# Gating the stream on GpSimd in the first phase, and adding x on TensorE in the projection

## The chip, the core and the metric

The kernel runs on one core of one Trainium2 chip. The core has five engines that each work through a list of instructions of their own: TensorE (PE in the profile, its weight loads PEld), VectorE (DVE), ScalarE (ACT), GpSimd (POOL) and SyncE (SP), which here issues most of the DMAs. They meet at semaphores. The metric is the device time of the whole kernel in microseconds; lower is better.

## What is computed

A layer with adaptive layer norm around two blocks: a full attention block, and two layers of local attention with a feed-forward part. B = 2, T = 2048, C = 256, so 32 tiles of 128 rows. The change is in the attention block's surroundings. Cut to what matters:

```python
mod = (_silu(L0_c) @ L0_wmod).reshape(L0_c.shape[0], 6, 1, -1)
sa, ca, ga, sb, cb, gb = (mod[:, k] for k in range(6))
ga = (2 * (ga >= 0) - 1) * jnp.maximum(jnp.abs(ga), 0.25)
h = _layernorm(x, axis=-1) * (1 + ca) + sa
x = x + ga * _L0_attn_ref(h, ...)            # attn(h) = h + out @ Wo.T
h = _layernorm(x, axis=-1) * (1 + cb) + sb
x = x + gb * _L0_ffn_ref(h, ...)             # two layers of local attention + feed-forward
```

So the stream behind the attention is x1 = x + ga * h + ga * (out @ Wo.T), and the input of the two layers is x2 = layernorm(x1) * (1 + cb) + sb. The product with ga in the last term sits in the weights: w_gated = Wo.T * ga.

## The kernel before

The 32 tiles are worked in 8 groups of 4 tiles (512 rows; a tile of a group in SBUF is 128 partitions x 4 x 256 numbers, 128x1024 in the profile). All data are float32. A float32 product on TensorE shows as two records in the trace. The phases run one after another, with a barrier between them: a short setup, the first phase (`qkv_phase`), the attention (`attention_phase`), the projection (`projection_phase`), and then for each of two layers a local attention and a feed-forward phase. Order within a phase is what the code writes for each engine: loops over groups, software-pipelined by hand, with a wait on a semaphore ahead of each step.

**First phase.** GpSimd loads a group of x (L284), then raises two variances to the power -0.5 (L287, 128x4). VectorE makes the statistics (L224, L229, L386), normalises (L393), multiplies and adds the modulation (L396, L401) to give h in `h_now`, makes its statistics (L404), normalises again into `hn` (L410). TensorE transposes `hn` (L332); ScalarE brings it back as `xnt` (L296) and copies h into `S.h1` (L298), which signals `h_kept`; VectorE waits for `h_kept` before it writes the next `h_now` (L401). TensorE makes the products for q and k (L343), v (L353) and the dot products (L363), VectorE rotates q and k (L418, L419, L424) and makes their low parts (L428). VectorE's list of a group n interleaves these: statistics of n + 1, then four rotations, with the steps `modulated`, `shifted` and `normed` (L393 to L410) of group n + 1 between them.

**Projection.** `S.h1` holds h. For each group n with buffer p = n mod 2: VectorE multiplies h by ga in place (L1092, `gate_x`, two groups ahead), GpSimd adds x, which SyncE fetched again into `x_again` (L1050, `add_x`, two groups ahead), TensorE multiplies the attention's output `ot` by `w_gated` into `y_ps` (L1080, two buffers), VectorE adds it (L1100, `residual`) and makes the statistics (L224, L229, L1105). GpSimd makes the power (L1054), VectorE the offset -mean * rstd (L1110, `centre`), ScalarE normalises (L1034), VectorE multiplies by 1 + cb (L1114, `modulate`), GpSimd adds sb (L1058, `shift`) into `S.x2`. SyncE sends x1 to HBM (L1011) behind each group's loads. Its list for group n is: wait for `x_added` of n - 2, fetch x (L1003), wait for `mm_done` of n - 2, fetch ot (L1007, two DMAs), wait for `x1_ready` of n - 2, send. ScalarE's queue loads the weights and tables of the next phase behind its second normalisation (`W.load_local`, L957 to L961).

Of the kernel before, what the change touches and what calls it, by code (L numbers as in the profile page):

```python
# [11 lines left out]
ALU = mybir.AluOpType  # L12
# [3 lines left out]
P = 128  # L16
# [216 lines left out]
def qkv_phase(nc, S, E, io):  # L233


    with ExitStack() as ctx:
# [23 lines left out]
        prime(nc, q)  # L260
        with nc.Block() as block:
# [18 lines left out]
            @block.gpsimd  # L280
            def _(pool):
                with pool.Fori(0, GROUPS) as n:
                    pool.wait_ge(q["x_used"], n + START)
                    pool.dma_start(xin[:, :, :], row_tiles(io["x"])[:, ds(n * GT, GT), :]).then_inc(x_in, 16)  # L284
                    for k, (given, done) in enumerate((("var1", "rstd1"), ("var2", "rstd2"))):
                        pool.wait_ge(q[given], n + 1 + START)
                        pool.tensor_tensor(rstd[:, k, :], var[:, k, :], S.half[:, 0:GT], ALU.pow).then_inc(q[done], 1)  # L287

            @block.scalar
            def _(act):  # L290
                def inputs(n):
# [6 lines left out]
                    act.activation(S.h1[:, ds(n * GT, GT), :], h_now[:, :, :], ACT.Copy).then_inc(q["h_kept"], 1)  # L298
# [75 lines left out]
            def _(dve):  # L374
                LINKS = 5

                def mod(n, s):
                    return S.mod[:, ds(n // GPB, 1), s, :].to_broadcast([P, GT, C])


# [591 lines left out]
def projection_phase(nc, S, W, io):  # L972

    with ExitStack() as ctx:
# [6 lines left out]
        offset, carrier = sb("offset", [P, 2, GT]), sb("carrier2", [P, 1])  # L981
        y_ps = ps("y_ps", [P, 2, GT, C])
        o_in, x_in = ([sem(f"p_{n}_in{k}") for k in range(2)] for n in "ox")
        names = "w w_ready x1_out x_gated x_added x1_ready mm_done var rstd offset_ready normed scaled x2_done chain".split()
# [11 lines left out]
        with nc.Block() as block:  # L996

            @block.sync
            def _(sp):
# [16 lines left out]
                with sp.Fori(1, GROUPS // 2) as i:  # L1016
                    for p in range(2):
                        n = 2 * i + p
                        sp.wait_ge(q["x_added"], n - 1 + START)
                        fetch_x(n, p)  # L1020
                        sp.wait_ge(q["mm_done"], n - 1 + START)
# [24 lines left out]
            def _(pool):  # L1046
                def add_x(n, p):
                    pool.wait_ge(x_in[p], 16 * (n // 2 + 1) + START)
                    pool.wait_ge(q["x_gated"], n + 1 + START)
                    pool.tensor_tensor(x1(n), x1(n), xin[:, p, :, :], ALU.add).then_inc(q["x_added"], 1)  # L1050

                def scale(n, p):
                    pool.wait_ge(q["var"], n + 1 + START)
                    pool.tensor_tensor(rstd[:, p, :], rstd[:, p, :], S.half[:, 0:GT], ALU.pow).then_inc(q["rstd"], 1)  # L1054

# [4 lines left out]
                add_x(0, 0)  # L1060
                add_x(1, 1)
                scale(0, 0)
                with pool.Fori(0, GROUPS // 2 - 1) as i:
                    for p in range(2):
                        n = 2 * i + p
                        add_x(n + 2, p)
# [7 lines left out]
            def _(pe):  # L1074
                def project(n, p, b):
                    pe.wait_ge(o_in[p], 16 * CC * (n // 2 + 1) + START)
                    pe.wait_ge(q["x1_ready"], n - 1 + P0 + START)
                    for t in range(GT):
                        for k in range(CC):
                            last = pe.matmul(y_ps[:, p, t, :], ot[:, p, k, t * P:(t + 1) * P], w_gated[:, b, k, :], start=k == 0, stop=k == CC - 1)  # L1080
# [9 lines left out]
            def _(dve):  # L1090
                def gate_x(n):
                    dve.tensor_tensor(x1(n), x1(n), mod(n, 2), ALU.mult).then_inc(q["x_gated"], 1)  # L1092

                def residual(n, p):
# [3 lines left out]
                    dve.wait_ge(q["x_added"], n + 1 + START)  # L1098
# [5 lines left out]
                                    lambda t: [S.h1[:, ds(n * GT + t, 1), :].rearrange("p t c -> p (t c)")]))  # L1104
                    dve.tensor_scalar(rstd[:, p, :], mv[:, p, :, 1], EPS, None, ALU.add).then_inc(q["var"], 1)  # L1105
                    c.closed()

                def centre(n, p):
                    dve.wait_ge(q["rstd"], n + 1 + START)
                    dve.scalar_tensor_tensor(offset[:, p, :], mv[:, p, :, 0], -1.0, rstd[:, p, :], ALU.mult, ALU.mult).then_inc(q["offset_ready"], 1)  # L1110
# [7 lines left out]
                gate_x(0)  # L1118
                gate_x(1)
# [815 lines left out]
```

## Time and profile before

| | us |
|---|---|
| median of 3 runs | 2889.11 |
| the runs | 2885.9 to 2897.32 |
| the profiled execution | 2896.74 |
| its span | 2894.7 |

Over the span TensorE is busy 88%, VectorE 76%, ScalarE 54% and GpSimd 19%. One execution was profiled; durations are read from it. Times on the axis are microseconds from the start of its span. In a timeline row the first number is the start, the second the busy time of the instructions on the row (x4 means four, merged), and square brackets hold the engine's idle time before them and what ended it.

### The profile page before, as it was taken

What the parts mean: (1) busy time and instruction counts of PE and PEld (TensorE: products, weight loads), DVE (VectorE), ACT (ScalarE), POOL (GpSimd) and SP (SyncE); (2) the same over time, 40 slices, a digit from 0 to 9 for tenths busy, and PEclk for the clock granted to TensorE, in tenths of its full rate; (3) what the DMA queues carried; (4) which work ended last, traced back from release to release, by engine and by line L of the source; (5) the groups of instructions that cost most, each with busy time, mean ns of one, the idle gap of its engine ahead of it and who ended that gap; (6) DMA issues with size and microseconds to landing.
All of it is one profiled execution on the core that took longest, in us unless ns stands there. A gap on an engine that the chain in (4) does not pass through costs nothing. (4 is left out here: it accounts for less than half of the span.)

```text
span 2894.7 us, 45406 instructions
## 1 busy us (share of the span) xinstructions
PE 2549.8 (88%) x14072; PEld 1542.4 (53%) x14072; DVE 2194.7 (76%) x4596; ACT 1558.3 (54%) x3447; POOL 563.3 (19%) x388
## 2 busy tenths in 40 slices
PE   4995999999999999943999999669969999995998
PEld 2443333333333333322677777458847777773877
DVE  4776999999999999846788888435558888883565
ACT  0221666766667667711666666434426666663443
POOL 0110010101101110134333333100013333330000
PEclk7997999999999999976999999889989999998999
DMA  2335244445444554244100000020020000001121
GB/s 85 110 110 140 84 134 109 124 127 141 119 112 124 127 138 118 75 160 133 51 9 9 9 8 7 30 101 17 15 60 9 8 9 9 9 4 37 57 62 40
DMA packets 123905, 204.92 MB, mean 71 GB/s; under 512 B 22560, under 2 KB 71008, under 8 KB 120400
## 3 DMA queue, kind: packets, MB, share of 16 engines
q1 hardware_dynamic: 109040, 163.96, 20.3%
q0 software_dynamic: 8832, 21.80, 2.6%
q10 hardware_dynamic: 5920, 17.75, 1.6%
q8 instruction: 58, 0.95, 0.1%
q14 instruction: 55, 0.45, 0.1%
HBM read 125.30 MB, written 54.26 MB: 62 GB/s over the span
## 5 line engine op out<-in xcount | busy, mean ns | idle before, releaser
L751 PE MATMUL o_ps<-probs,vx 128*33 128x512 f32 (+3 forms) x2560 | 545.4, 548 | 0.0
L802 ACT ACTIVATE probs<-st_ps 128x512 f32<-128x512 f32 (+3 forms) x640 | 339.2, 530 | 314.3 <-PE st_ps L736 180.7
L853 DVE SCALAR_TENSOR_TENSOR geo_x<-geo_rows,kp_t 128x512 f32<-128x512 f32 (+3 forms) x640 | 437.7, 708 | 4.0 <-ACT probs L804 4.0
L832 DVE TENSOR_REDUCE chunk_max<-a_ps 128x1 f32<-128x512 f32 (+3 forms) x640 | 358.9, 602 | 41.9 <-PE a_ps L719 35.3
L804 ACT ACTIVATE probs<-geo_x 128x512 f32<-128x512 f32 (+3 forms) x640 | 360.9, 564 | 12.9 <-DVE geo_x L859 12.9
L1227 PE MATMUL local_in_ps<-w_local,local_ht 128*128 128x512 f32 x1152 | 322.5, 417 | 9.7 <-ACT local_sq L1369 5.3
L1388 ACT ACTIVATE local_probs<-local_s_ps,local_bias,local_inv 128x256 f32<-128x256 f32 x512 | 282.6, 563 | 13.9 <-DVE local_bias L1483 13.9
L1663 PE MATMUL ff_ag_ps<-ff_ht_parts,w 128*128 128x512 f32 (+1 forms) x1056 | 259.9, 405 | 33.6 <-DVE ff_gate L1772 25.4
L719 PE MATMUL a_ps<-k,q 96*128 96x512 f32 (+3 forms) x640 | 237.6, 445 | 43.3 <-DVE chunk_max L832 35.6
L1395 ACT ACTIVATE local_pt<-local_pt_ps 128x512 f32<-128x512 f32 x256 | 152.4, 596 | 208.9 <-PE local_pt_ps L1285 200.8
L751 PEld LDWEIGHTS o_ps<-probs,vx 128*33 128x33 f32 x2560 | 124.2, 112 | 260.4 <-issue 186.9
L719 PEld LDWEIGHTS a_ps<-k,q 96*128 96x128 f32 x640 | 108.9, 198 | 266.4 <-DVE chunk_max L832 135.7
L1479 DVE TENSOR_REDUCE local_top<-local_s_ps 128x4 f32<-128x1024 f32 x128 | 156.8, 1225 | 122.3 <-PE local_s_ps L1271 122.3
L1663 PEld LDWEIGHTS ff_ag_ps<-ff_ht_parts,w 128*128 128x128 f32 (+1 forms) x1056 | 200.0, 192 | 88.7 <-DVE ff_gate L1772 33.8
L1227 PEld LDWEIGHTS local_in_ps<-w_local,local_ht 128*128 128x128 f32 x1152 | 207.6, 193 | 58.2 <-issue 18.8
L1490 DVE TENSOR_SCALAR local_probs<-local_probs,local_rden 128x256 f32<-128x256 f32 x512 | 223.0, 477 | 9.0
L1556 POOL TENSOR_TENSOR local_inv<-local_norm,half 128x16 f32<-128x16 f32 x64 | 186.4, 2912 | 174.9 <-DVE local_norm L1468 107.6
L734 PE MATMUL st_ps<-q,k 98*128 98x512 f32 (+3 forms) x640 | 217.8, 412 | 2.0 <-DMA q<-maxima 2.0
L1676 PE MATMUL ff_y_ps<-ff_w,ff_act_t 128*128 128x256 f32 x1152 | 149.6, 285 | 14.5 <-DVE ff_act_t L1778 13.8
L1295 PE MATMUL local_o_ps<-local_pt,local_v_ring 128*64 128x128 f32 x2048 | 154.6, 282 | 3.3 <-ACT local_pt L1395 3.1
L1285 PE MATMUL local_pt_ps<-ident,local_probs 128*128 128x128 f32 x1024 | 150.7, 280 | 6.2 <-DVE local_probs L1490 1.4
L1676 PEld LDWEIGHTS ff_y_ps<-ff_w,ff_act_t 128*128 128x128 f32 x1152 | 140.5, 190 | 21.2 <-DVE ff_act_t L1778 21.0
(171 smaller groups left out, 3848.8 us busy)
## 6 DMA issues: line engine op xcount, KB each, us to landing
geo_rows<-geo SPq DMA_DIRECT2D x64, 512.0 KB, 7.5
q<-q_parts SPq DMA_DIRECT2D x48, 256.0 KB, 4.2
k<-k_parts SPq DMA_DIRECT2D x48, 256.0 KB, 6.3
piece_lo<-in_pieces POOLq DMA_DIRECT2D x15, 768.0 KB, 5.9
weight_parts<-piece_hi SPq DMA_DIRECT2D x15, 768.0 KB, 3.4
weight_parts<-piece_lo SPq DMA_DIRECT2D x15, 768.0 KB, 6.0
raw<-out_t SPq DMA_DIRECT2D x128, 64.0 KB
shares_in<-shares SPq DMA_DIRECT2D x64, 128.0 KB, 4.6
```

The source lines that it names most:

```text
L719: ins = pe.matmul(slot[:, 0:width], q3[s][0:ROWS, it * P:(it + 1) * P], k3[s][0:ROWS, c * GTOK:c * GTOK + width], start=True, stop=not diag)
L734: ins = pe.matmul(out[:, off:GTOK], k3[s][:, j * P:(j + 1) * P], q3[s][:, g * GTOK + off:(g + 1) * GTOK], start=True, stop=not diag)
L751: ins = pe.matmul(o_ps[kind * HALF:kind * HALF + VW, g % 2, off:GTOK], vx[s][:, j, :], probs[:, i % PSLOTS, kind, off:GTOK], start=j == 0, ...
L802: act.activation(probs[:, s % PSLOTS, 0, off:GTOK], st_ps[:, (b * NB + s) % STBANKS, off:GTOK], ACT.Exp).then_inc(q["st_used"], 1)
L804: act.activation(probs[:, s % PSLOTS, 1, off:GTOK], geo_x[:, s % GSLOTS, off:GTOK], ACT.Exp).then_inc(q["probs_ready"], 1)
L832: dve.reduce_max(chunk_max[:, it, c:c + 1], a_ps[:, n % ABANKS, 0:width], AX.X).then_inc(q["a_used"], 1)
L853: ins = dve.scalar_tensor_tensor(out[:, off:GTOK], geo[:, 1, at], kp_t[:, j, ds(b, 1)].rearrange("p o -> p o"), geo[:, 0, at], ALU.add, AL ...
L1227: last = pe.matmul(in_ps[:, j, :], ht[:, p, a, k, :], w[:, b, k, j * INNER:(j + 1) * INNER], start=i == 0, stop=i == len(steps) - 1)
L1388: last = act.activation(probs[:, hd, :], s_ps[:, a, x % 2 * 2 * P:(x % 2 + 1) * 2 * P], ACT.Exp, bias=bias[:, hd:hd + 1], scale=inv[:, p, ...
L1490: last = dve.tensor_scalar(probs[:, hd, :], probs[:, hd, :], rden[:, hd:hd + 1], None, ALU.mult)
L1663: last = pe.matmul(ag_ps[0:rows, x % 2, half, :], w1[:, a, k, c0:c0 + rows], ht_parts[:, b, k, :], start=i == 0, stop=i == len(steps) - 1)
L1676: last = pe.matmul(y_ps[:, t, :], act_t[:, a, x, t * P:(t + 1) * P], w2[:, b, x, :], start=(x, i) == (0, 0), stop=x == HC - 1 and i == len ...
```

## The change

In the first phase ScalarE's copy of h into `S.h1` goes. In its place GpSimd multiplies `h_now` by ga into `S.h1` (`keep_gated`), in its list behind the load of the next group's x; the last group's stands behind the loop. `h_kept` is now signalled by it.

In the projection VectorE's `gate_x` and GpSimd's `add_x` go, with their semaphores. TensorE adds x: two products of the identity with `x_again` (128x512 each) open the accumulation in `y_ps`, and the products with `ot` go on in it. SyncE fetches x for group n behind `mm_done` of n - 2, with ot. The offset is made in two steps: VectorE writes -mean to `centre` (128x4), GpSimd multiplies it by rstd right behind the power.

```diff
             @block.gpsimd
             def _(pool):
-                with pool.Fori(0, GROUPS) as n:
+                def fetch(n):
                     pool.wait_ge(q["x_used"], n + START)
                     pool.dma_start(xin[:, :, :], row_tiles(io["x"])[:, ds(n * GT, GT), :]).then_inc(x_in, 16)
+
+                def scales(n):
                     for k, (given, done) in enumerate((("var1", "rstd1"), ("var2", "rstd2"))):
                         pool.wait_ge(q[given], n + 1 + START)
                         pool.tensor_tensor(rstd[:, k, :], var[:, k, :], S.half[:, 0:GT], ALU.pow).then_inc(q[done], 1)
+
+                def keep_gated(n):
+                    pool.wait_ge(q["h_ready"], n + 1 + START)
+                    pool.tensor_tensor(S.h1[:, ds(n * GT, GT), :], h_now[:, :, :], mod(n, 2), ALU.mult).then_inc(q["h_kept"], 1)
+
+                fetch(0)
+                scales(0)
+                with pool.Fori(1, GROUPS) as n:
+                    fetch(n)
+                    keep_gated(n - 1)
+                    scales(n)
+                keep_gated(GROUPS - 1)
...
-                    act.activation(S.h1[:, ds(n * GT, GT), :], h_now[:, :, :], ACT.Copy).then_inc(q["h_kept"], 1)
...
-                        sp.wait_ge(q["x_added"], n - 1 + START)
+                        sp.wait_ge(q["mm_done"], n - 1 + START)
                         fetch_x(n, p)
-                        sp.wait_ge(q["mm_done"], n - 1 + START)
                         fetch_o(n, p)
                         send(n - 2)
...
                 def scale(n, p):
                     pool.wait_ge(q["var"], n + 1 + START)
                     pool.tensor_tensor(rstd[:, p, :], rstd[:, p, :], S.half[:, 0:GT], ALU.pow).then_inc(q["rstd"], 1)
+                    pool.wait_ge(q["rstd"], n + 1 + START)
+                    pool.tensor_tensor(offset[:, p, :], centre[:, p, :], rstd[:, p, :], ALU.mult).then_inc(q["offset_ready"], 1)
...
-                        add_x(n + 2, p)
                         scale(n + 1, 1 - p)
                         shift(n, p)
...
                 def project(n, p, b):
+                    pe.wait_ge(x_in[p], 16 * (n // 2 + 1) + START)
+                    pe.wait_ge(q["x1_ready"], n - 1 + P0 + START)
+                    for t in range(0, GT, 2):
+                        pe.matmul(y_ps[:, p, t:t + 2, :], S.ident[:, :], xin[:, p, t:t + 2, :], start=True, stop=False)
                     pe.wait_ge(o_in[p], 16 * CC * (n // 2 + 1) + START)
-                    pe.wait_ge(q["x1_ready"], n - 1 + P0 + START)
...
-                            last = pe.matmul(y_ps[:, p, t, :], ot[:, p, k, t * P:(t + 1) * P], w_gated[:, b, k, :], start=k == 0, stop=k == CC - 1)
+                            last = pe.matmul(y_ps[:, p, t, :], ot[:, p, k, t * P:(t + 1) * P], w_gated[:, b, k, :], start=False, stop=k == CC - 1 and t % 2 == 1)
...
                     dve.wait_ge(q["normed"], n - 1 + P0 + START)
-                    dve.wait_ge(q["x_added"], n + 1 + START)
                     dve.wait_ge(q["mm_done"], n + 1 + START)
...
+                    dve.tensor_scalar(centre[:, p, :], mv[:, p, :, 0], -1.0, None, ALU.mult)
                     dve.tensor_scalar(rstd[:, p, :], mv[:, p, :, 1], EPS, None, ALU.add).then_inc(q["var"], 1)
...
-                        gate_x(n + 2)
-                        centre(n, p)
                         residual(n + 1, 1 - p)
                         modulate(n, p)
```

GpSimd in the first phase, before: the loop over groups is a load of x and two powers (an ISA row sets a register or a configuration).

```order
L282 ISA
L284 ISA
L284 DMA xin<-in_x 128x4x256
L286 REGISTER_ALU
L287 ISA
L287 TENSOR_TENSOR rstd<-var,half 128x4 x2
L282 REGISTER_ALU
L282 COMPARE_AND_BRANCH
```

The same loop after, with the instruction that follows it (line numbers are those of the changed file; x is S.h1).

```order
L300 ISA
L287 ISA
L287 DMA xin<-in_x 128x4x256
L296 ISA x2
L296 TENSOR_TENSOR x<-h_now,mod 128x1024
L291 REGISTER_ALU
L292 TENSOR_TENSOR rstd<-var,half 128x4 x2
L300 REGISTER_ALU
L300 COMPARE_AND_BRANCH
L296 TENSOR_TENSOR x<-h_now,mod 128x1024
```

A 128x1024 multiply now stands between the load and the two powers, and one more behind the loop.

GpSimd in the projection, before: the first half of the loop's body (x on L1050 is S.h1, on L1058 S.x2).

```order
L1050 ISA
L1050 TENSOR_TENSOR x<-x,x_again 128x1024
L1053 REGISTER_ALU
L1054 TENSOR_TENSOR rstd<-rstd,half 128x4
L1058 ISA x2
L1058 TENSOR_TENSOR x<-normed,mod 128x1024
```

And after:

```order
L1059 TENSOR_TENSOR rstd<-rstd,half 128x4
L1061 TENSOR_TENSOR offset<-centre,rstd 128x4
L1064 REGISTER_ALU
L1065 ISA x2
L1065 TENSOR_TENSOR x<-normed,mod 128x1024
```

The addition of x is gone and a 128x4 multiply stands behind the power.

TensorE in the projection after, the two halves of the loop's body; before there were only the groups of eight.

```order
L1083 MATMUL y_ps<-x_again,ident 128x512 x2
L1084 ISA
L1087 MATMUL y_ps<-w_gated,ot 128x256 x8
L1080 ISA
L1081 REGISTER_ALU
L1083 MATMUL y_ps<-x_again,ident 128x512 x2
L1084 ISA
L1087 MATMUL y_ps<-w_gated,ot 128x256 x8
```

Each group of eight products with `ot` now has two 128x512 products ahead of it.

## Rows read from the trace of the kernel before

**Rows 1.** Projection: busy us of PE, PEld, DVE, ACT, POOL; clock, DMA share, GB/s:

```profile
1265.00:1349.00 84.00, 34.15 (x128) 27.36 (x128) 62.97 (x124) 16.61 (x32) 52.40 (x24) 0.72 0.64 224
```

**Rows 2.** Timeline, one group of the first phase: start, us, instructions:

```profile
80.65 14.00 PE L343 MATMUL qk_ps<-xnt,w_qkv 128*128 128x512 f32 x32
...
84.57 0.69 DVE L418 SCALAR_TENSOR_TENSOR rot_c<-qk_ps,cos_t 128x512 f32<-128x512 f32 x1 [4.11 <-PE qk_ps L343]
...
95.43 1.01 POOL L287 TENSOR_TENSOR rstd<-var,half 128x4 f32<-128x4 f32 x1 [13.86 <-DVE var L404]
...
96.41 0.80 POOL L284 DMA_DIRECT2D xin<-in_x  x1
...
97.18 0.68 DVE L428 TENSOR_TENSOR lo<-qk,hi 128x512 fp32r<-128x512 f32 x1
...
97.78 1.38 DVE L410 TENSOR_SCALAR hn<-h_now,mv,rstd 128x256 f32<-128x256 f32 x4
...
102.80 1.88 PE L363 MATMUL v_ps<-qk,dirs 128*8 128x512 f32 x4 [1.42 <-ACT dots_sb L316]
...
104.61 1.98 PE L343 MATMUL qk_ps<-xnt,w_qkv 128*128 128x512 f32 x4
```

**Rows 3.** Groups to 290 us: xcount, busy us, mean ns, idle before:

```profile
L410 DVE TENSOR_SCALAR hn<-h_now,mv,rstd 128x256 f32<-128x256 f32 x32 | 11.1, 409 | 1.1 <-POOL rstd L287 1.1
...
L214 DVE SCALAR_TENSOR_TENSOR mag<-mod 128x256 f32<-128x256 f32 x4 | 1.7, 426 | 0.1
...
L215 DVE TENSOR_SCALAR mag<-mag 128x256 f32<-128x256 f32 x4 | 1.2, 294 | 0.1
```

**Rows 4.** Two lines of VectorE: shortest, median and longest ns of one:

```profile
L1110 DVE SCALAR_TENSOR_TENSOR offset<-mv,rstd x8: 155/2297/2308, 1283.6 to 1340.3; 128x4 f32<-128x4 f32 x8
...
L1490 DVE TENSOR_SCALAR local_probs<-local_probs,local_rden x512: 340/352/1458, 1384.9 to 2629.6; 128x256 f32<-128x256 f32 x171
```

**Rows 5.** Timeline, local attention, VectorE and GpSimd side by side:

```profile
1512.80 1.72 DVE L1490 TENSOR_SCALAR local_probs<-local_probs,local_rden 128x256 f32<-128x256 f32 x2
...
1512.82 1.30 POOL L1550 TENSOR_TENSOR local_qk_nat<-local_rot_c,local_rot_s 128x512 f32<-128x512 f32 x1 [4.89 <-PE local_pt_ps L1248]
```

**Rows 6.** Timeline of the projection, one group:

```profile
1291.48 1.21 DVE L1100 TENSOR_TENSOR x<-x,y_ps 128x1024 f32 x1
...
1291.50 2.36 POOL L1050 TENSOR_TENSOR x<-x,x_again 128x1024 f32 x1
...
1296.86 2.48 POOL L1058 TENSOR_TENSOR x<-normed,mod 128x1024 f32 x1
...
1297.06 2.30 DVE L1110 SCALAR_TENSOR_TENSOR offset<-mv,rstd 128x4 f32<-128x4 f32 x1
...
1299.28 1.21 DVE L1100 TENSOR_TENSOR x<-x,y_ps 128x1024 f32 x1
```

**Rows 7.** Timeline of the projection, TensorE's products and the first L1100:

```profile
1272.22 9.63 PE L1080 MATMUL y_ps<-w_gated,ot 128*128 128x256 f32 x32 [32.64 <-DMA ot<-o_t]
...
1278.54 1.22 DVE L1100 TENSOR_TENSOR x<-x,y_ps 128x1024 f32<-128x1024 f32 x1 [9.03 <-PE y_ps L1080]
...
1313.13 13.46 PE L1080 MATMUL y_ps<-w_gated,ot 128*128 128x256 f32 x48 [16.67 <-DMA ot<-o_t]
```

**Rows 8.** Projection DMAs: KB each, us to landing; first load's issue:

```profile
w_local<-weight_parts ACTq DMA_DIRECT2D x2, 1536.0 KB, 8.5
...
table<-in_xpos ACTq DMA_DIRECT2D x4, 512.0 KB, 14.2
...
1291.60 0.93 ACTq L957 DMA_DIRECT2D w_local<-weight_parts  x2
```

**Rows 9.** Timeline of the projection's end:

```profile
1335.04 1.21 DVE L1100 TENSOR_TENSOR x<-x,y_ps 128x1024 f32<-128x1024 f32 x1
...
1340.35 2.30 DVE L1110 SCALAR_TENSOR_TENSOR offset<-mv,rstd 128x4 f32<-128x4 f32 x1 [0.91 <-POOL rstd L1054]
...
1346.19 2.34 POOL L1058 TENSOR_TENSOR x<-normed,mod 128x1024 f32<-128x1024 f32 x1 [3.56 <-DVE normed L1114]
```

More of the change, by code:

```diff
@@ L260, in qkv_phase, with mod @@
         prime(nc, q)
+        def mod(n, s):
+            return S.mod[:, ds(n // GPB, 1), s, :].to_broadcast([P, GT, C])
         with nc.Block() as block:
@@ L375, in _ @@
                 LINKS = 5
-                def mod(n, s):
-                    return S.mod[:, ds(n // GPB, 1), s, :].to_broadcast([P, GT, C])
                 def statistics(n):
@@ L980, in projection_phase @@
         stats, mv, rstd = sb("stats2", [P, GT, 1, 6]), sb("mv2", [P, 2, GT, 2]), sb("rstd2", [P, 2, GT])
-        offset, carrier = sb("offset", [P, 2, GT]), sb("carrier2", [P, 1])
+        centre, offset, carrier = sb("centre2", [P, 2, GT]), sb("offset", [P, 2, GT]), sb("carrier2", [P, 1])
         y_ps = ps("y_ps", [P, 2, GT, C])
         o_in, x_in = ([sem(f"p_{n}_in{k}") for k in range(2)] for n in "ox")
-        names = "w w_ready x1_out x_gated x_added x1_ready mm_done var rstd offset_ready normed scaled x2_done chain".split()
+        names = "w w_ready x1_out x1_ready mm_done var rstd offset_ready normed scaled x2_done chain".split()
         q = {n: sem("p_" + n) for n in names}
@@ L1046, in _ @@
             def _(pool):
[L1047 to L1050, printed above, removed]
                 def scale(n, p):
@@ L1058, in shift @@
                     pool.tensor_tensor(S.x2[:, ds(slot(n * GT), GT), :], normed[:, p, :, :], mod(n, 3), ALU.add).then_inc(q["x2_done"], 1)
-                add_x(0, 0)
-                add_x(1, 1)
                 scale(0, 0)
@@ L1090, in _ @@
             def _(dve):
-                def gate_x(n):
-                    dve.tensor_tensor(x1(n), x1(n), mod(n, 2), ALU.mult).then_inc(q["x_gated"], 1)
                 def residual(n, p):
@@ L1104, in residual @@
                                     lambda t: [S.h1[:, ds(n * GT + t, 1), :].rearrange("p t c -> p (t c)")]))
+                    dve.tensor_scalar(centre[:, p, :], mv[:, p, :, 0], -1.0, None, ALU.mult)
                     dve.tensor_scalar(rstd[:, p, :], mv[:, p, :, 1], EPS, None, ALU.add).then_inc(q["var"], 1)
                     c.closed()
-                def centre(n, p):
-                    dve.wait_ge(q["rstd"], n + 1 + START)
-                    dve.scalar_tensor_tensor(offset[:, p, :], mv[:, p, :, 0], -1.0, rstd[:, p, :], ALU.mult, ALU.mult).then_inc(q["offset_ready"], 1)
                 def modulate(n, p):
@@ L1117, in _ @@
                 dve.memset(S.x2[:, XS, :], 0.0)
-                gate_x(0)
-                gate_x(1)
                 dve.wait_ge(q["w"], 16 + START)
@@ L1127, in _ @@
                         n = 2 * i + p
-                        gate_x(n + 2)
-                        centre(n, p)
                         residual(n + 1, 1 - p)
                         modulate(n, p)
-                centre(GROUPS - 2, 0)
                 residual(GROUPS - 1, 1)
                 modulate(GROUPS - 2, 0)
-                centre(GROUPS - 1, 1)
                 modulate(GROUPS - 1, 1)
```

## The prediction

> **What bounds the kernel now.** I read busy times by stage first. The change edits two stages, the first phase (35 to 245 us) and the projection (1265 to 1349 us, 84 us long, [rows 1]: no engine is full there, and TensorE's granted clock averages 0.72); nothing between or behind them is edited. The profiled run took 2896.74 us with a span of 2894.7, so 2.0 us lie outside; the median of the three runs is 2889.11, 7.6 us below it. I work out a difference from the profiled execution and put it on the median.
>
> First phase, by the timeline of one group [rows 2]. From one first product of L343 to the next (80.65 to 104.61) is 23.96 us. The chain is: TensorE makes the first product, VectorE waits 4.11 us for it (84.57), and is then busy without a gap to the end of its list: rotations, statistics, then the normalisation L410 at 97.78, the last rotation, and after that ScalarE's copies and TensorE's L363, which waited 1.42 us for them (102.80), then L343 again. So a delay of VectorE between 84.57 and 101 lengthens the group by as much. ScalarE's copy L298, which goes away, comes behind the copies that L343 needs and runs beside L343's products: taking it away is worth 0.
>
> Projection [rows 6]: a group takes 7.80 us (1291.48 to 1299.28), set by VectorE with GpSimd. L1110, on 128x4 numbers, takes 2.30 us, because it starts at 1297.06 behind GpSimd's L1058 (1296.86, 2.48 us) and ends with it. TensorE has 16 records of half the width of L343's, which take 14.00/32 = 0.44 us each [rows 2]: 3.7 us with a little between them. Once in the phase another thing ends last: TensorE waits 16.67 us for ot (until 1313.13), which is queued with the weights that ScalarE's queue loads from 1291.60 on [rows 7, 8].
>
> **The lock.** Does GpSimd hold up VectorE in the first phase too? In rows 5 GpSimd adds two 128x512 tiles in SBUF for 1.30 us, and VectorE's pair of L1490 beside it (a TENSOR_SCALAR from SBUF to SBUF) takes 1.72 us; the longest single one is 1458 ns against a median of 352 [rows 4], so it waits about 1.1 us. That is GpSimd's time less 0.2. L1110 tells the same: a median of 2297 ns against a shortest of 155 [rows 4], under an operation of 2.33 to 2.48. Is L410 of that kind? It has two scalars taken from tiles, where L1490 has one. By duration it is: L214, with two SBUF inputs, takes 426 ns for 256 columns, L215 and L410, with one, 294 and 409 [rows 3]. L410 is shorter than a pass of one column at a time although it also fetches two scalars, so I take it as running on both read paths, like L215 and L1490. No row shows L410 itself under a large GpSimd operation: the ends for it are 0 and the whole operation, 2.48 us. The Trainium skill says in "SBUF — State Buffer", section "SBUF: two separate sides", that a VectorE operation in a two-port mode or with two SBUF inputs and a GpSimd operation exclude each other for the whole instruction; by it L410 would wait, which speaks against this change, and the sum would be the one below; without it the first phase would lose nothing. The rows of L1490 agree with it.
>
> **Part 1: L298's copy becomes GpSimd's multiply in the first phase.** The new instruction is one 128x1024 TENSOR_TENSOR a group, 8 in all, of the form of L1058 (2.33 us without a wait). It stands behind the load of the next x: in rows 2 that load's issue is over at 96.41 + 0.80 = 97.21. VectorE's L428, two SBUF inputs, starts at 97.18 and runs to 97.86; GpSimd gets its turn when that ends, and L410, due at 97.78, finds it taken until about 100.2. By the two rows above that costs 2.33 less 0.18 = 2.15 us, on the chain. The rotations that follow read PSUM and one tile, as L1100 does, which ran 1.21 us under L1050 [rows 6]. For the eighth group no load stands between: the multiply starts right behind the power, and blocks L424 instead, two SBUF inputs, for the same price. Behind the multiply on GpSimd stands only the next power, due when the next group's statistics are through, and VectorE's wait of L401 for h_kept is half a group later: neither is late. Sum: 8 x 2.15 = 17 us lost. Ends: 0 and 8 x 2.48 = 20.
>
> **Part 2: the projection.** VectorE loses L1092 (1.22 us) and L1110 (2.30), gets a 128x4 TENSOR_SCALAR (0.17). GpSimd loses L1050 (2.36) and gets a 128x4 multiply; the power of the same shape takes 1.01 [rows 2], and a 1024-column addition 2.36 against 1.30 for 512 columns [rows 5, 6] leaves 0.2 us for one without columns: I take 0.2. TensorE gets two 128x512 products a group, 4 records of 14.00/32 = 0.44 us [rows 2]: 1.75 us, so 3.7 + 1.75 = 5.5 us a group. VectorE then has 7.80 - 1.22 - 2.30 + 0.2 = 4.5 us and GpSimd 2.0 (a power behind VectorE's multiply) + 0.2 + 2.4 = 4.6. TensorE becomes the longest, at 5.5.
>
> Were that all, the eighth group's products would end at about 1278.3 (the first group's end, as now [rows 7], since its x product fills the wait for ot) + 7 x 5.5 = 1317, against 1335.04 for the start of L1100 now [rows 9]; with the tail below, 20 us gained. But the loads don't allow it. (a) x for group n is now fetched after the products of group n - 2 and not when x was added, so x and ot come together about 5 us later: group 2 starts some 2 us later than now, and x and ot of group 4 are asked for at 1289.5. (b) ScalarE's loads start behind its second normalisation, 2 us sooner than now (1291.60 [rows 8]), at about 1289: w_local is 2 x 1536 KB, the tables 4 x 512 KB, together 5.1 MB, plus 0.5 MB. So now group 4 falls among them too, where before it had its data. (c) The bytes stay the same, and so does when ScalarE's and these loads are through: x and ot of group 5 land near 1313 to 1315, as now (TensorE's wait ended at 1313.13 [rows 7]). Group 5 then takes 5.5 us on a clock that is low at first (4 records of 128x512 more; the first 32 records took 9.63 us instead of 7.4 [rows 7]), so its products end at about 1320; only then are x and ot of group 7 asked for, 5 to 6 us to landing; group 7's products end at about 1331.5, against 1335.04 where L1100 starts now: 3.5 us gained.
>
> The tail: from L1100 at 1335.04 to the end of L1058 at 1348.53 is 13.5 us [rows 9]. In it L1110 sits 2.30 us behind GpSimd's addition of group 6. The offset now stands ahead of that addition, in 0.2 us and one more semaphore: 2 us gained, 11.5 left. Together 3.5 + 2 = about 6 us gained (rounded up, since group 6 also waits for less). Ends: 20 us, when TensorE alone sets the pace, and -3, when the fetches behind mm_done come in series on a low clock.
>
> **Sum.** +17 - 6 = +11 us: 2889.1 + 11 = 2900 us. About 0.5%, 14.4 us, is what a measurement of this kernel can tell from no change, so this is "no change", on the slow side.
>
> **Rivals.**
> 1. L410 isn't held up, or GpSimd's multiply starts only after 99.2, when the four of L410 are through. For: no row shows a two-scalar TENSOR_SCALAR blocked; against: its duration, and that 1.9 us of register work would have to stand between. The first phase loses 0 to 2: 2889 - 6 + 1 = 2884. Chance 0.12.
> 2. The loads collide less than I say: group 4's x and ot are through before w_local's rows are in the queues, and TensorE's 5.5 us set the pace up to there and after. For: the new order issues them half a microsecond before. Gain in the projection 12 to 16 instead of 6, first phase +17: 2889 + 17 - 14 = 2892. Chance 0.14.
> 3. **Slower.** TensorE's fetch chain eats the gain. Place: x and ot of groups 6 and 7 are each asked for behind mm_done of 4 and 5, while TensorE sits at the low clock, where 4 more records cost 3.5 us and not 1.75. When the two last groups each cost 3 us more than I counted, nothing of the 6 us remains; it decides from a gain of under 2.6 us in the projection, with the first phase at +17: 2889 + 17 + 1 = 2907. Chance 0.18.
> 4. Both 1 and the full 20 us of the projection: 2869. Chance 0.03.
> The forecast keeps 0.53, from 2893 to 2904.
>
> **Range and chances.** 2885 to 2908 holds the forecast, rivals 2 and 3 and half of rival 1, each with some us for the runs' own spread (2885.9 to 2897.3); left out are rival 4, half of rival 1 and the outer end of 3. Faster by over 0.5% (under 2874.7): rival 4 and a little of 1, 0.05. Slower by over 0.5% (over 2903.6): rival 3 and the upper edge of the forecast, 0.22. Within: 0.73.
>
> **What would show it.** In the timeline of the first phase the first instruction of L410 lasts over 2.4 us in seven groups, and a group takes 26.1 us instead of 23.96. In the projection the wait of TensorE for ot appears before group 4 as well as before 5, the small scaling on VectorE no longer lasts 2.3 us, and the phase ends 6 us sooner after its start. I am wrong if groups of the first phase stay at 24 us (rival 1), if TensorE has no wait of over 5 us before group 4 (rival 2), or if the last products end after 1334 on the old time axis (rival 3).

## The result, and the profile after

| | before | after |
|---|---|---|
| median of the runs, us | 2889.11 | 2914.39 |
| the runs, us | 2885.9 to 2897.32 | 2911.89 to 2916.28 |
| the profiled execution and its span, us | 2896.74, 2894.7 | 2916.28, 2914.2 |

The changed kernel takes 1.0083 times the time of the kernel before (95% interval 1.006 to 1.0105), 25.3 us more: slower by more than the interval leaves open, and above the predicted range (2885 to 2908 us). Between the two profiled executions the difference of the spans is 19.5 us, since the profiled execution of before lay 7.6 us above its median and that of after 1.9. By phases (from VectorE's first instruction of one to that of the next):

| phase | before, us | after, us | difference |
|---|---|---|---|
| first phase | 223.21 | 253.88 | +30.7 |
| attention (not edited) | 1007.24 | 1003.74 | -3.5 |
| projection | 83.58 | 74.57 | -9.0 |
| first local attention (not edited) | 511.13 | 513.51 | +2.4 |
| start and the phases behind | | | -1.0 |

The two edited phases together are 21.7 us longer; the other 3.6 us of the timed 25.3 stand in no edited phase.

The windows view of after over these four phases; the columns are the stretch, its length, the busy time and count of each engine, TensorE's granted clock, and the DMA engines' share. The third row answers to [rows 1].

```profile
core 0: us, PE busy (x) PEld busy (x) DVE busy (x) ACT busy (x) POOL busy (x), PEclk, DMA share, GB/s
34.68:288.56 253.88, 194.42 (x513) 87.82 (x514) 175.21 (x375) 47.41 (x80) 43.72 (x36) 0.87 0.26 86
288.56:1292.30 1003.74, 929.09 (x4416) 367.59 (x4416) 916.85 (x1813) 651.92 (x1390) 107.50 (x110) 0.95 0.45 117
1292.30:1366.87 74.57, 47.67 (x160) 33.06 (x160) 37.10 (x117) 16.51 (x32) 34.19 (x24) 0.80 0.70 252
1366.87:1880.38 513.51, 484.74 (x3328) 350.68 (x3328) 391.95 (x873) 327.76 (x832) 177.00 (x98) 0.97 0.06 15
```

**First phase.** The timeline of after, one group, answering to [rows 2]. Lines have moved: L439 is the former L428 (low part), L421 is L410 (normalisation), L348 the transposes (L332), L379 the dot products (L363), L359 is L343, L429 is L418. L296 is GpSimd's new multiply.

```profile
74.76 0.82 POOL L287 DMA_DIRECT2D xin<-in_x  x1
...
75.54 2.99 DVE L439 TENSOR_TENSOR lo<-qk,hi 128x512 fp32r<-128x512 f32 x1
75.61 2.37 POOL L296 TENSOR_TENSOR x<-h_now,mod 128x1024 f32 x1
...
76.83 1.88 PE L379 MATMUL v_ps<-qk,dirs_q 128*8 128x512 f32 x4 [0.37 <-ACT values L324]
...
78.45 1.37 DVE L421 TENSOR_SCALAR hn<-h_now,mv,rstd 128x256 f32<-128x256 f32 x4
...
79.97 1.09 PE L348 MATMUL tp<-ident,hn 128*128 128x128 f32 x8 [1.26 <-DVE hn L421]
...
83.46 3.57 PE L379 MATMUL v_ps<-qk,dirs 128*8 128x512 f32 x4 [2.40 <-ACT dots_sb L332]
...
86.96 14.79 PE L359 MATMUL qk_ps<-xnt,w_qkv 128*128 128x512 f32 x32
...
91.67 0.69 DVE L429 SCALAR_TENSOR_TENSOR rot_c<-qk_ps,cos_t 128x512 f32<-128x512 f32 x1 [6.59 <-PE qk_ps L359]
```

The multiply starts where the prediction put it, right behind the load of x (74.76 + 0.82). But the instruction held up is the one that VectorE has already begun: the low part L439 lasts 2.99 us where it takes 0.68, and L421 runs its four in 1.37 us, undisturbed. That is 2.31 us of hold-up, and it should make a group 26.3 us. From one L359 to the next it is 28.0 to 28.5 in the five groups from 86.96 on; the first takes 30.2 where it took 25.9, and the last, whose multiply meets another instruction (below), 26.2. The rest stands in the rows of TensorE: its wait before L379 is 2.40 us where it was 1.42 [rows 2], L379 then takes 3.57 us where it took 1.88, and VectorE waits 6.59 us for L359's first product where it waited 4.11. TensorE also has a new wait of 1.26 us ahead of the transposes (L348). The windows view of the same place shows why:

```profile
80.00:81.00 1.00, 1.00 (x8) 0.82 (x8) 1.00 (x2) 0.00 (x0) 0.00 (x0) 1.00 0.00 0
81.00:82.00 1.00, 0.06 (x1) 0.00 (x0) 0.97 (x3) 0.22 (x1) 0.00 (x0) 0.88 0.00 0
82.00:83.00 1.00, 0.00 (x0) 0.00 (x0) 0.91 (x2) 1.00 (x3) 0.00 (x0) 0.50 0.00 0
...
84.00:85.00 1.00, 1.00 (x2) 0.13 (x1) 0.92 (x8) 0.68 (x2) 0.00 (x0) 0.50 0.44 166
...
87.00:88.00 1.00, 1.00 (x3) 0.48 (x3) 0.00 (x0) 0.59 (x1) 0.00 (x0) 0.50 1.03 356
88.00:89.00 1.00, 1.00 (x3) 0.50 (x2) 0.00 (x0) 0.00 (x0) 0.00 (x0) 0.71 1.05 395
89.00:90.00 1.00, 1.00 (x3) 0.38 (x2) 0.00 (x0) 0.00 (x0) 0.00 (x0) 1.00 1.05 393
```

TensorE stops at 81.06 (transposes done); from 82 to 88 its granted clock is 0.50 (1.2 of 2.4 GHz), from 89 on 1.00. In the kernel before the same place, with a pause of 1.42 us, is at 1.00 throughout. Over all of 60 to 236 us the granted clock is 1.00 before and 0.92 after.

Why does a hold-up of VectorE by 2.31 us lengthen a pause of TensorE by only 0.98? Before, the first dot product kept TensorE busy until 100.29, 1.2 us into VectorE's last rotation; after, it runs during the hold-up (76.83), so that the transposes start 0.2 us into the rotation and are done 1 us earlier against it, while the second dot product still waits for that rotation.

Durations of L439 and L421 (min/median/max, ns), the second answering to [rows 3]. Six of L439's 32 are long, by 2.31 us each. The one long L421 is in the first group, and it is held up as well, by 2.9 us:

```profile
L439 DVE TENSOR_TENSOR lo<-qk,hi x32: 678/684/2996, 69.8 to 271.5; 128x512 fp32r<-128x512 f32 x32
```

```profile
L421 DVE TENSOR_SCALAR hn<-h_now,mv,rstd x32: 398/401/3277, 49.5 to 248.6; 128x256 f32<-128x256 f32 x32
```

```profile
49.55 4.25 DVE L421 TENSOR_SCALAR hn<-h_now,mv,rstd 128x256 f32<-128x256 f32 x4 [1.13 <-POOL rstd L292]
...
50.31 2.35 POOL L296 TENSOR_TENSOR x<-h_now,mod 128x1024 f32 x1
```

The record of the first of these four starts 0.76 us ahead of the multiply's, and ends behind it. The eighth multiply (244.25) meets L435, the former L424, as the prediction said; it lasts 2.74 us where it takes 0.69.

**Projection.** Timeline of after, answering to [rows 6, 7, 9]: L1083 are the products with x, L1087 those with ot (the former L1080), L1061 the offset on GpSimd, L1103 the addition (L1100). Groups are counted from 0, as in the prediction.

```profile
1297.29 3.47 PE L1083 MATMUL y_ps<-x_again,ident 128*128 128x512 f32 x4 [31.09 <-DMA x_again<-in_x]
...
1308.87 0.20 POOL L1061 TENSOR_TENSOR offset<-centre,rstd 128x4 f32<-128x4 f32 x1
...
1315.29 0.95 ACTq L968 DMA_DIRECT2D w_local<-weight_parts  x2
...
1319.55 1.88 PE L1083 MATMUL y_ps<-x_again,ident 128*128 128x512 f32 x4
1319.90 0.38 SPq L1014 DMA_DIRECT2D x_again<-in_x  x1
...
1323.52 5.41 PE L1087 MATMUL y_ps<-w_gated,ot 128*128 128x256 f32 x16 [2.09 <-DMA ot<-o_t]
...
1336.52 3.78 PE L1083 MATMUL y_ps<-x_again,ident 128*128 128x512 f32 x4 [7.59 <-DMA x_again<-in_x]
...
1354.75 1.22 DVE L1103 TENSOR_TENSOR x<-x,y_ps 128x1024 f32<-128x1024 f32 x1 [0.52 <-PE y_ps L1087]
```

Groups 1 to 4 follow each other in 5.17 us, as TensorE's products take. The fetches then collide with ScalarE's loads (first issue at 1315.29; from 1320 to 1337 the DMA engines' share is 0.97 to 1.02): group 4 waits 2.09 us for ot, and group 5 waits 7.59 us for x, asked for at 1319.90 and used 16.6 us later. Group 3's x, asked for at 1309.56, was used 4.8 us later. The last addition starts 62.5 us into the phase, where it was 69.5, and the tail is 12.1 us instead of 14.1.

### The profile page after: what moved, and what is told of

Same layout as the page of the kernel before. It is cut to its first block and busy times, and to the rows that moved or that the text cites. A ratio compares the mean times of both kernels' runs of the same rounds, so it can differ in the third digit from the quotient of the medians.

```text
span 2914.2 us, 45429 instructions
## 1 busy us (share of the span) xinstructions
PE 2574.1 (88%) x14104; PEld 1550.4 (53%) x14104; DVE 2187.4 (75%) x4588; ACT 1551.6 (53%) x3439; POOL 562.5 (19%) x396
```

## The experiments

Ratios are to the kernel before on the same chip; its medians there were 2899.29 us (e1 to e4), 2897.54 (e5, e7, e8, b1) and 2893.88 (e6, e9 to e11). Where no ratio stands, there was one run (e4 to e7, e9, b1), and the phases of its trace are what counts. "Before" in a comparison of phases is the first trace of the kernel before.

### One part at a time: e1_gate_only, e2_proj_only, b1_before_again

e1 has the first phase of after, and before's projection without L1092 (`gate_x`). e2 has before's first phase; in the projection x is added by TensorE and the offset made by GpSimd, and VectorE keeps its `gate_x`.

```diff
 # e1, against before: keep_gated in the first phase, and
-                        gate_x(n + 2)
-                    pool.wait_ge(q["x_gated"], n + 1 + START)
 # e2, against after's projection:
+                        gate_x(n + 2)
+                    dve.wait_ge(q["x_gated"], n + 1 + START)
```

> Theory A (the whole loss is in the first phase: GpSimd's multiply holds VectorE up for 2.3 us a group, and TensorE's longer pause then lets its clock fall): the first phase lasts 254 us as in the changed kernel, 30 us over before, and the projection gains only what the gate on VectorE cost, 8 x 1.2 us at most and less for the waits on loads, 3 to 8 us. Total 20 to 27 us slower than before. Rival B (the loss needs the two parts together, since the changed projection or the new layout of semaphores moves the phases between): under 10 us slower.

Measured: 2930.54 us, ratio 1.0103 (1.0078 to 1.0129), so about 30 us slower where 20 to 27 was expected. The first phase took 252.40 us (+29.2), the projection 84.45 (+0.9).

> First phase as before, gate left on VectorE in the projection, x added by TensorE and offset made by GpSimd. Theory A: first phase 223 us, projection 75 to 79 us against 83.6 before, total 5 to 9 us faster than before. Rival B (part of the loss comes from the changed projection, by way of the phase behind it, which was 2.4 us longer): no gain, 0 to 3 us.

Measured: 2898.65 us, ratio 0.9995 (0.997 to 1.0021). First phase 223.18 us, projection 80.10 (-3.5), where 75 to 79 was expected: a miss, and no gain in the whole.

The loss of the edited phases is all in the first. In the projection the parts don't add up: taking the gate off VectorE alone gives nothing (a gain of 3 to 8 was expected), x and the offset without it give 3.5, all three together 9.0. So the gate is worth nothing by itself and 5.5 us on top of the other two.

b1 is the kernel before once more, for how much a phase varies by itself.

> The kernel before, unchanged, profiled a second time, to see how much the phases that nothing edits vary by themselves. Expected: first phase 223, projection 83 to 84 us, each within 1 us of the first profile; the attention phase between 1001 and 1025 us, longer by about half of the time that the granted clock stood at its lower level in it. If it varies by under 3 us, the differences between the kernels in that phase are their own.

Measured: 2902.02 us; first phase 223.01, attention 1013.51 (1007.24 in the first trace), projection 83.87, local attention 512.72. The edited phases repeat within 0.3 us; the attention does not. The changed projection repeats less well: the same code took 74.57 us in after, 74.58 in e4 and 75.61 in e3, so a difference of 1 us there says nothing.

### The first phase: e3_moved, e4_filled, e5_delay

e3 puts the multiply between the two powers of the next group, where VectorE sits waiting for the products, and the last one behind the seventh group's last low part (`scale(n, k)` is one of the two powers of `scales(n)`).

```diff
-                    keep_gated(n - 1)
-                    scales(n)
-                keep_gated(GROUPS - 1)
+                    scale(n, 0)
+                    keep_gated(n - 1)
+                    scale(n, 1)
+                pool.wait_ge(q["lo_done"], 4 * (GROUPS - 1) + START)
+                keep_gated(GROUPS - 1)
```

> The changed kernel with GpSimd's multiply moved between the two powers of the next group, where VectorE waits 4.1 us for TensorE, and the last one behind the last low part but four. Theory A: no instruction of VectorE is held up, the clock stays at its upper level, the first phase is back at 223 us, and the kernel is 9 to 13 us faster than before (2876 to 2880 on the scale of the median of before). Rival C (GpSimd's multiply or its longer list costs the first phase something wherever it stands, by memory traffic or by its semaphore): first phase 230 us or more, and the kernel no faster than before.

Measured: 2895.4 us, ratio 0.9978 (0.9964 to 0.9992). First phase 222.69 us (-0.5), projection 75.61 (-8.0). The whole gained 4 us where 9 to 13 was expected; the two edited phases account for 8.5, and the attention took 1020.52 us in this trace. Timeline of e3, the multiply beside VectorE's idle time:

```profile
79.17 1.02 POOL L292 TENSOR_TENSOR rstd<-var,half 128x4 f32<-128x4 f32 x1 [7.28 <-DVE var L400]
...
80.18 2.33 POOL L296 TENSOR_TENSOR x<-h_now,mod 128x1024 f32 x1
...
83.20 0.69 DVE L432 SCALAR_TENSOR_TENSOR rot_c<-qk_ps,cos_t 128x512 f32<-128x512 f32 x1 [4.12 <-PE qk_ps L362]
```

The multiply (80.18 to 82.51) lies inside VectorE's wait of 4.12 us, which ends at 83.20. GpSimd's work is that of after, and the 30 us are gone: the place did it.

e4 leaves the multiply where after has it, and gives TensorE something to do in its pause: two products of the identity with the cosines ahead of the second dot product, into a part of PSUM that is written anew. They are not part of what is computed.

```diff
                         if u and more:
                             transposed(n + 1)
+                            for _ in range(2):
+                                pe.matmul(qk_ps[:, 0, 0, :], S.ident[:, :], cos[:, 0:512], start=True, stop=True)
```

> The changed kernel with two products of the identity with a table, 1.75 us in all, ahead of the second dot product of each group in the first phase, where TensorE waits 2.4 us. They only keep TensorE at work; their result is overwritten. Theory A, with two causes added up (hold-up 2.3 us a group, clock the rest): the granted clock stays at 1.00 there, groups take 26.3 us instead of 28.75, the first phase 235 to 238 us. Rival D (the whole 4.8 us a group is the hold-up by GpSimd, the clock costs nothing): groups stay at 28.7 us or grow by the 1.75.

Measured: 2924.16 us; first phase 241.56 us (+18.35), where 235 to 238 was expected, attention 1024.87, projection 74.58. Timeline of e4:

```profile
74.16 2.99 DVE L441 TENSOR_TENSOR lo<-qk,hi 128x512 fp32r<-128x512 f32 x1
74.23 2.36 POOL L296 TENSOR_TENSOR x<-h_now,mod 128x1024 f32 x1
...
79.52 1.88 PE L376 MATMUL qk_ps<-cos_t,ident 128*128 128x512 f32 x4
...
82.08 1.88 PE L381 MATMUL v_ps<-qk,dirs 128*8 128x512 f32 x4 [0.69 <-ACT values L324]
...
235.09 1.88 PE L381 MATMUL v_ps<-qk,dirs_q 128*8 128x512 f32 x4 [2.42 <-ACT values L324]
```

The hold-up is there as in after (2.99 us), the added products (L376) fill the pause, TensorE waits 0.69 us instead of 2.40, and the second dot product (L381) takes 1.88 us again; the granted clock over 60 to 236 us is 1.00, and a group takes 26.3 us. What remains is 18.35 us, against 8 x 2.31 = 18.5. So the clock's share in after's loss is 253.88 - 241.56 = 12.3 us. The length of one pause doesn't decide by itself: at the eighth multiply of e4 (235.09) TensorE waits 2.42 us and the granted clock stays at 1.00, while at the same place of after it falls right behind such a wait (the dot product at 248.34 takes 2.96 us; 0.50 from 249 on). Filling the pause before the second dot product was enough to keep it there; whether the new wait of 1.26 us ahead of the transposes is needed for the fall, no run separates.

e5 asks whether it needs GpSimd at all: the kernel before, with a VectorE memset of 2560 columns (2.19 us) ahead of L410, and no work added to GpSimd.

```diff
                     dve.wait_ge(q["xt_ready"], CC * n + START)
+                    dve.memset(pad[:, :], 0.0)
                     for t in range(GT):
                         last = dve.tensor_scalar(hn
```

> The kernel before, with a memset of 2560 columns of an unused tile (about 2.3 us on VectorE) ahead of each normalisation of the first phase; GpSimd does nothing new. Theory A: what counts is that VectorE is 2.3 us late there, whoever is to blame, so groups take 28.7 us as in the changed kernel, TensorE's clock is low at each group's first products, and the first phase lasts 251 to 255 us. Rival E (the clock falls or the products slow down because of GpSimd's own traffic): groups take 26.3 us, the phase 240 to 243 us.

Measured: 2936.63 us; first phase 257.91 us (+34.7), projection 82.37. Timeline of e5 (L364 is the dot product, L410 the memset):

```profile
83.48 3.57 PE L364 MATMUL v_ps<-qk,dirs 128*8 128x512 f32 x4 [2.40 <-ACT dots_sb L317]
...
86.99 14.62 PE L344 MATMUL qk_ps<-xnt,w_qkv 128*128 128x512 f32 x32
...
91.53 0.69 DVE L420 SCALAR_TENSOR_TENSOR rot_c<-qk_ps,cos_t 128x512 f32<-128x512 f32 x1 [6.43 <-PE qk_ps L344]
...
105.30 2.19 DVE L410 MEMSET pad<- 128x2560 f32 x1 [0.48 <-issue]
```

The same wait of 2.40 us, the same 3.57 us for the dot product, and a granted clock of 0.91 over 60 to 236 us. A delay of VectorE alone brings the clock down; GpSimd's multiply isn't needed for it. It cost somewhat more than expected (8 x 2.19 = 17.5 us for the memsets, 17.2 for the rest), and 4.0 us more than after: here the last of the groups is as long as the others (six of 28.1 to 28.9 us), where after's took 26.2.

### The projection: e6_offset_dve, e7_x_pool

Both are e3 with one part of the projection undone: the offset back on VectorE (e6), or x added by GpSimd and fetched behind that addition, with no identity products (e7). The main lines of each:

```diff
 # e6
-                    pool.tensor_tensor(offset[:, p, :], centre[:, p, :], rstd[:, p, :], ALU.mult).then_inc(q["offset_ready"], 1)
+                    dve.scalar_tensor_tensor(offset[:, p, :], mv[:, p, :, 0], -1.0, rstd[:, p, :], ALU.mult, ALU.mult).then_inc(q["offset_ready"], 1)
 # e7
+                        add_x(n + 2, p)
-                        pe.matmul(y_ps[:, p, t:t + 2, :], S.ident[:, :], xin[:, p, t:t + 2, :], start=True, stop=False)
```

> e3_moved with the offset back on VectorE (a 128x4 instruction ahead of each addition of the product), so gate moved away and x added by TensorE, but not the third part. The runs so far gave, for the projection: before 83.6 us, gate away alone 84.4, x and offset 80.1, gate and offset 74.5, all three 74.6 to 75.6. Theory H (the offset behind GpSimd's addition of the shift holds VectorE up for 2.3 us a group and is what the other two parts are worth nothing without): 80 to 84 us. Rival I (TensorE's addition frees GpSimd, so the offset no longer waits): 75 to 78 us.

Measured: 2893.74 us; projection 82.95 us, 7.3 more than e3 and 0.6 less than before. Timeline of e6:

```profile
1293.51 2.34 POOL L1066 TENSOR_TENSOR x<-normed,mod 128x1024 f32 x1
1293.56 2.31 DVE L1114 SCALAR_TENSOR_TENSOR offset<-mv,rstd 128x4 f32<-128x4 f32 x1 [0.91 <-POOL rstd L1062]
```

VectorE waits 0.91 us for the power, and then its 128x4 instruction is held up for all of GpSimd's addition, as in the kernel before; from 1285.91 to the next of these it is 7.65 us.

> The kernel with the moved multiply (e3_moved), but x added by GpSimd as before, TensorE without the two identity products, x fetched behind x_added. The first phase stays at 223 us. If adding x on TensorE is what shortens the projection: 80 us or more here against 75.6. If it is the gate and the offset, and the identity products only cost: 72 to 76 us. I expect 78 to 82, since GpSimd then has 7 us of work a group with its hold-ups, against TensorE's 5.2.

Measured: 2893.71 us; projection 74.45 us, as in after (74.57), where 78 to 82 was expected: a miss. So adding x on TensorE was worth nothing here, and the gain needs the other two together: without the offset 0.6 us are left of it (e6), without the gate 3.5 (e2). The offset alone was not run.

### The fetches: e8_loads_late, e9_loads_4, e10_loads_5, e11_x_pool_loads_5

If the fetches set the end, moving ScalarE's loads of the next phase must show it. All are e3 with `W.load_local` moved from behind the second normalisation: behind the last (e8), the fourth (e9) or the sixth (e10); e11 is e10 with GpSimd adding x, as in e7. The lines are e10's, against e3.

```diff
-                W.load_local(act, S, io, 0)
-                with act.Fori(1, GROUPS // 2) as i:
+                with act.Fori(1, GROUPS // 2 - 1) as i:
                     for p in range(2):
                         normalise(2 * i + p, p)
+                W.load_local(act, S, io, 0)
+                for p in range(2):
+                    normalise(GROUPS - 2 + p, p)
```

> e3_moved with the loads of the next phase's weights and tables behind the last normalisation instead of behind the second. Theory F (these loads are what TensorE waits for in groups 4 and 5 of the projection, by sharing the DMA engines): no wait over 2 us for x or ot, the projection takes 64 to 68 us instead of 75.6; the local attention behind it waits for its weights and takes up to 12 us more. Rival G (the fetches behind mm_done are late by themselves): the projection stays above 72 us. In total 0 to 8 us faster than e3_moved, or up to 5 slower if the weights come later than the first products of the next phase, which start 15 us after its start anyway.

Measured: 2888.19 us, ratio 0.9963 (0.995 to 0.9976). Projection 64.46 us (-19.1 against before), but the local attention took 520.11 (+9.0): its own first fetches (`local_h_in`) now run among these loads. In the kernel before the first product of the local attention starts 10.1 us into that phase (not 15, as the expectation has it); in e8 16.8 us (the phase begins at 1338.45), by its timeline:

```profile
1355.29 0.69 PE L1212 MATMUL local_in_ps<-ident,local_h_in 128*128 128x128 f32 x2 [31.79 <-DMA local_h_in<-x]
```

> e3_moved with the next phase's loads behind the fourth normalisation. Theory F: the loads then share the DMA engines with the fetches of groups 6 and 7 only; projection 68 to 73 us, and the phase behind it 511 to 514, since the weights land before its first product. Rival: the same 75 us, with the wait moved to group 6 or 7.

Measured: 2888.76 us; projection 80.60 us (-3.0), where 68 to 73 was expected: a miss. The collision moved two groups back, and the clock fell with it:

```profile
1312.30 3.78 PE L1089 MATMUL y_ps<-x_again,ident 128*128 128x512 f32 x4 [7.17 <-DMA x_again<-in_x]
...
1324.86 3.77 PE L1089 MATMUL y_ps<-x_again,ident 128*128 128x512 f32 x4 [4.56 <-DMA x_again<-in_x]
```

Two waits for x (7.17 and 4.56 us), and behind each the products at the low clock (3.78 us for four that otherwise take 1.88).

> e3_moved with the next phase's loads behind the sixth normalisation. Theory F: all fetches but the last are out of their way; projection 64 to 67 us as with the loads at the very end (64.5), and the phase behind it 513 to 517 us, since they start 10 us sooner than there, where it took 520. Total 2 to 6 us faster than with the loads at the end, 0.994 to 0.995 of before.

Measured: 2875.8 us, ratio 0.9932 (0.9911 to 0.9954). Projection 64.89 us (-18.7), local attention 511.58 (+0.5). The windows row of e10's projection, and TensorE's last group with the first load:

```profile
1262.42:1327.31 64.89, 45.03 (x160) 31.55 (x160) 38.78 (x117) 16.52 (x32) 34.34 (x24) 0.84 0.80 281
```

```profile
1307.46 1.88 PE L1088 MATMUL y_ps<-x_again,ident 128*128 128x512 f32 x4
...
1308.18 0.41 ACTq L971 DMA_DIRECT2D w_local<-weight_parts  x1
```

By the time the first load is issued (1308.18) the products of the eighth group (group 7) have begun (1307.46). This version beats both kernels: 18 us under before on the same chip, and by the ratios (0.9932 and 1.0083) clearly under after.

> The same loads, and x added by GpSimd as before, TensorE without the identity products. With the loads out of the way the projection's pace is that of the busiest engine: GpSimd, whose list a group is 2.35 + 2.0 + 0.2 + 2.35 = 6.9 us, against TensorE's 5.2 in e10_loads_5. Projection 70 to 74 us, so 5 to 8 us more than e10_loads_5. If it is within 2 us of it, adding x on TensorE is worth nothing even then.

Measured: 2886.09 us, ratio 0.9974 (0.9959 to 0.9989). Projection 71.54 us. A group takes 7.1 us, set by GpSimd. Timeline of e11, GpSimd over one group (L1065 adds x, L1069 is the power, L1071 the offset, L1075 adds sb), and TensorE beside it:

```profile
1305.12 2.35 POOL L1065 TENSOR_TENSOR x<-x,x_again 128x1024 f32 x1
1305.17 3.38 DVE L1125 TENSOR_TENSOR normed<-normed,mod 128x1024 f32<-128x1024 f32 x1
...
1307.43 2.00 POOL L1069 TENSOR_TENSOR rstd<-rstd,half 128x4 f32<-128x4 f32 x1
...
1309.51 0.20 POOL L1071 TENSOR_TENSOR offset<-centre,rstd 128x4 f32<-128x4 f32 x1
...
1309.97 2.34 POOL L1075 TENSOR_TENSOR x<-normed,mod 128x1024 f32 x1 [0.26 <-issue]
...
1312.27 2.35 POOL L1065 TENSOR_TENSOR x<-x,x_again 128x1024 f32 x1
...
1312.92 3.72 PE L1097 MATMUL y_ps<-w_gated,ot 128*128 128x256 f32 x16 [3.34 <-DMA ot<-o_t]
```

GpSimd goes from one instruction to the next; the power takes 2.00 us instead of 1.01 while VectorE's multiply (L1125, two SBUF inputs, itself held up by L1065) runs to 1308.55, which fits a wait for it. Now that the loads are out of the way, x on TensorE is worth 71.54 - 64.89 = 6.6 us. The same edit is worth nothing or 6.6 us, depending on what else bounds the phase.

## Why the prediction was wrong

**The mechanism of the first phase was right, its size was short by the clock.** The sum held 8 x 2.15 = 17 us for VectorE's hold-up; it measured 2.31 in six groups, 2.9 in the first and 2.05 in the last, and e4, which has the hold-up without the low clock, lost 18.35. That term stands. In six groups the instruction was another: the prediction let L428 finish first and L410 wait; L428 itself waited, although by the trace it had started 0.07 us before the multiply. On a chain without a gap it doesn't matter which waits, but rival 1, that L410 might not be held up, was thus for six groups a question about the wrong instruction. In the first group it was asked of the right one, and the answer is that it is held up (3.28 us instead of 0.40). The Trainium skill's "SBUF — State Buffer", section "SBUF: two separate sides", says that whichever of the two starts first gets the shared ports for its whole instruction; the trace does not agree for these starts (75.54 and 75.61), nor does it in [rows 5], where VectorE's record starts 0.02 us ahead and is the longer one. In the first group VectorE's record even starts 0.76 us ahead (49.55 and 50.31) and waits. The measurement decides: who starts first in the trace doesn't tell who has to wait.

**The step that failed** is what is late behind the hold-up. The prediction followed VectorE's delay to "the group is longer by as much" and priced what comes behind at nothing. TensorE's wait before the second dot product grew from 1.42 to 2.40 us, its granted clock fell to 0.50 in that pause, and it paid in the dot product and the first products of the next group: 28.0 to 28.5 us a group instead of 26.3, and 12.3 us in all (e4). GpSimd's multiply is not needed for it (e5). Without these 12.3 us the time would have been about 2902, inside the range. The profile before held the warning: [rows 2] show a TensorE wait of 1.42 us, and [rows 7] what the first products after an idle time cost (9.63 us instead of 7.4). That term was asked for in the projection and not in the first phase.

**The copy of ScalarE** was worth 0, as said: e3's first phase without it took 222.69 us against 223.21.

**The projection** gained 9.0 us where 6 was forecast, inside the ends given. The tail was right (2.0 us; GpSimd's offset at 0.20 us as estimated). The wait of over 5 us before group 4 did not come (2.09); group 5 began 44.2 us into the phase and not as late as before (47.6), so the last products gave 7.0 and not 3.5. The collision with the loads that held back the 20 us was real: e10 takes it away and gains 18.7. But the credit was spread wrongly: x on TensorE gained nothing while loads collide (e7). The gate off VectorE gained nothing alone (e1: 0.9 us longer) and 5.5 us with the other two (e2 against after), and without the offset nearly all of the gain is gone (e6), since it stands 2.3 us behind GpSimd's addition again.

**The rivals.** Rival 3, the one on the slower side, had its place in the projection and did not happen. The loss came from a place where no rival stood. Rivals 1 and 4 fell with the hold-up. The sign of rival 2 did appear, no wait of over 5 us before group 4, but its gain of 12 to 16 us did not: the collision came one group later and left 9.0.

**What stays open.** The timed medians differ by 25.3 us and the two profiled executions by 19.5, of which the edited phases are 21.7 and the others -2.2. The attention, in which nothing was edited, took 1001 to 1025 us in the 14 traces, by and large longer the more time TensorE had at the low clock (by the clock's record 93.5 us low in e2's 1001.5, 147.6 in e4's 1024.9); differences of a few us between single executions can't be put down to an edit. Why it varies wasn't tried.

## What to carry to other kernels

When an edit delays an engine on the chain, look up what TensorE waits for behind it: a pause that grows can cost on top of the delay (here 12.3 us on 18.4), because the products behind it may run at half the clock. Put a large GpSimd operation on SBUF where VectorE waits anyway (here the same multiply cost 30 us in one place and nothing in another). When three edits shorten one phase, ask what ends it, here the fetches behind another queue's loads, since only then does it show which edit is worth anything.

## What the runs showed of the hardware

- A VectorE instruction that by the trace began 0.07 us before GpSimd's 128x1024 multiply waited for all of it: 2.99 us instead of 0.68. A TENSOR_SCALAR with two scalars from tiles is held up too: it began 0.76 us before the multiply and took 3.28 us instead of 0.40.
- TensorE's granted clock fell to 0.50 in a pause of 2.40 us and was still there at 88, with TensorE at work since 83.46; with a pause of 1.42 us at the same place it stayed at 1.00. Two extra products in the pause kept it up and saved 12.3 us, although e4 has another pause of 2.42 us (235.09), in which it stayed at 1.00 too.
- Loads on another queue set how long a fetch takes: in after a fetch of x that was asked for at 1319.90, among ScalarE's loads, was used 16.6 us later, the one of 1309.56, ahead of them, 4.8 us later. Moved by four normalisations (e10), the same loads cost next to nothing in either phase; moved by two (e9), they cost 5.0 us more than where they were (one trace each).
